# A graph layer on one core: 25 units instead of 21, 24 gathered blocks instead of 28, hand-overs set farther apart, and an opening in another order

## The reference

```python
h = jnp.maximum(_layernorm(x, axis=-1), 0.0)        # x: 12500 nodes x 128, float32
msgs = h[src]                                       # 200000 edges, sorted by dst
agg = jax.ops.segment_sum(msgs, dst, num_segments=n)
deg = jax.ops.segment_sum(jnp.ones((src.shape[0],), h.dtype), dst, num_segments=n)
agg = agg / jnp.maximum(deg, 1.0)[:, None]
h = jax.nn.relu(agg @ Wg + h @ Ws + bg)             # 128 -> 128
h = jnp.tanh(h @ W1 + b1)                           # 128 -> 512
h = jnp.tanh(h @ W2 + b2)                           # 512 -> 512
return x + (h @ W3 + b3)                            # 512 -> 128
```

## Time and profile before

| | us |
|---|---|
| median of 3 runs | 1642.91 |
| profiled execution | 1658.69 |
| its span, first to last instruction | 1656.8 |
| TensorE busy | 1257.9 (76%) |
| VectorE busy | 956.5 (58%) |
| GpSimd busy | 897.7 (54%) |
| ScalarE busy | 552.8 (33%) |

### The profile page before, as it was taken

The page is one execution under the profiler, slowest core; times in us unless marked ns, Lnnn a source line. Parts: engine busy times, 40 slices in busy tenths (PEclk is TensorE's granted clock), DMA queues, the critical chain, the costliest instruction groups (busy, mean ns, idle before and its releaser), DMA issues.

```text
span 1656.8 us, 26502 instructions
## 1 busy us (share of the span) xinstructions
PE 1257.9 (76%) x9082; PEld 924.4 (56%) x9082; DVE 956.5 (58%) x1850; ACT 552.8 (33%) x1159; POOL 897.7 (54%) x953
## 2 busy tenths in 40 slices
PE   0204988778887888877888788888887888887888
PEld 0202656556665656565655555666555656565667
DVE  8806985546555575646556574547555665546441
ACT  6303441414142341414142341424142432324152
POOL 4473165656555655656566554656555554565530
PEclk9557999999989999888999999999988889899999
DMA  9611224142413314141414313141313313141410
GB/s 244 190 51 62 79 62 100 49 99 64 87 42 100 94 44 99 45 99 41 104 49 100 92 46 93 47 102 44 103 45 101 91 45 94 47 102 43 101 41 10
DMA packets 92829, 130.44 MB, mean 79 GB/s; under 512 B 47451, under 2 KB 73393, under 8 KB 88993
## 3 DMA queue, kind: packets, MB, share of 16 engines
q1 hardware_dynamic: 63773, 69.42, 16.3%
q0 software_dynamic: 28928, 59.30, 14.4%
HBM read 109.14 MB, written 13.09 MB: 74 GB/s over the span
## 4 chain that ended last, share of the span: by engine, by line
PE 54%; another core or an unknown queue 18%; issue 12%; ACT 8%; DVE 6%; DMA 1%; DVEq 0%; SPq 0%; ACTq 0%
PE banks L870 16%; PE banks L816 14%; PE banks L741 7%; PE banks L832 5%; PE banks L853 4%; PE banks L887 4%; DVE arena L1584 3%; ACT arena L1204 2%; ACT dense L1187 2%; ACT arena L1125 1%; PE banks L844 1%; PE banks L847 1%; ACT dense L1194 1%; PE banks L789 1%
## 5 line engine op out<-in xcount | busy, mean ns | idle before, releaser
L669 POOL DMA_INDIRECT ring<-h_table,idx_all x904 | 875.6, 969 | 670.3 <-issue 235.7
L870 PE MATMUL banks<-dense,w 128*128 128x256 f32 (+1 forms) x1568 | 430.5, 392 | 30.1 <-ACT dense L1194 16.8
L816 PE MATMUL banks<-xin,arena 128*128 128x256 f16 x2058 | 313.5, 287 | 103.9 <-issue 61.3
L1204 ACT CAST arena<-banks 128x512 f16<-128x512 f32 (+1 forms) x525 | 291.7, 579 | 206.2 <-PE banks L816 129.8
L870 PEld LDWEIGHTS banks<-dense,w 128*128 128x128 f32 x1568 | 272.2, 197 | 76.7 <-ACT dense L1194 20.8
L816 PEld LDWEIGHTS banks<-xin,arena 128*128 128x128 f16 x2058 | 190.3, 102 | 217.8 <-issue 117.4
L741 PE MATMUL banks<-ring,onehot 128*128 (+1 forms) x1008 | 194.6, 290 | 23.9 <-issue 18.1
L1574 DVE TENSOR_SCALAR arena<-arena,code_ptr 128x768 f16<-128x768 f16 (+1 forms) x336 | 133.6, 456 | 119.0 <-PE banks L816 89.6
L1584 DVE TENSOR_TENSOR arena<-node,banks 128x768 f16<-128x768 f16 (+1 forms) x168 | 152.5, 965 | 45.9 <-remote 24.7
L1194 ACT ACTIVATE dense<-banks,b2c 128x256 f32<-128x256 f32 (+1 forms) x196 | 92.0, 475 | 243.5 <-PE banks L870 125.7
L832 PE MATMUL banks<-arena 64*128 64x257 f16 x2058 | 146.5, 288 | 27.1 <-issue 21.5
(11 more groups left out here) (121 smaller groups left out, 871.2 us busy)
## 6 DMA issues: line engine op xcount, KB each, us to landing
arena<-unit_codes SPq DMA_DIRECT2D x21, 1568.0 KB
ring<-h_table,idx_all POOLq DMA_INDIRECT x904
xblk<-in_x_dram SPq DMA_DIRECT2D x48, 128.0 KB
out_dram<-dense SPq DMA_DIRECT2D x48, 128.0 KB
xin<-in_x_dram SPq DMA_DIRECT2D x4, 1232.0 KB, 17.0
h_table<-xin SPq DMA_DIRECT2D x4, 1232.0 KB
own_pair<-h_table SPq DMA_TRANSPOSE x98
w<-in_L_gnn_W_dram SPq DMA_DIRECT2D x1, 1024.0 KB
```

Of the source, the lines that this page charges most:

```text
L669: nc.gpsimd.indirect_dma_start(out=ring_tiles[:, t % RING, 0:2 * D], out_offset=None, in_=table, in_offset=bass.IndirectOffsetOnAxis(ap=id ...
L816: mm = nc.tensor.matmul(to, wide_l[:, piece % WSLOTS, k, j, :], tab[:, row_of(g, j), :], start=(j == 0), stop=(j == 1))
L870: mm = nc.tensor.matmul(l3_ps[c][:, 0:w], w2[:, q, c * P:(c + 1) * P], h2T[:, q, 0:w], start=(q == 0), stop=(q == HC - 1))
L1204: nc.scalar.copy(unit_msgs[:, 2 * pr:2 * pr + wide_of, 0:2 * D], unit_ps[pr % 2][:, 0:wide_of * 2 * D].rearrange("p (g d) -> p g d", d=2 * ...
```

## The change

- PB goes from 28 to 24, so there are 25 units and 24 GpSimd blocks, and no extra blocks. Units 2 to 24 have regular periods but for period 2 and the last.
- LOT_NS is 1200, and `due` is always the clock of the last hand-over plus 1200, never less.
- OPEN_LOTS is 24. Behind the first FIRST_LOTS = 12 gathers GpSimd waits for `qlT_ready`, which ScalarE raises when unit 0's codes are ready, then issues 12 more.
- The opening: unit 0 is gathered and summed, its dense layers run at once (`first_block`) with the first two steps of GpSimd's sums, and unit 1 is prepared behind them; the first GpSimd block's layers run with the gather of unit 1 (`first_gather`); then unit 1's block with the gather of unit 2 (`period_alone(2)`).
- VectorE's work of the opening follows the same order. The splitting of the remaining source indices (`split_sources(1)`) moves behind unit 0's block.

```diff
-OPEN_LOTS = 48
-LOT_NS = 1000
+FIRST_LOTS = 12
+OPEN_LOTS = 24
+LOT_NS = 1200
-PB = 28
-EXTRA_BEHIND = (2, 4, 7, 9, 12, 14, 17, 19)
+PB = 24
+EXTRA_BEHIND = ()
+PAIRS_FIRST = (0, 0, 0, 0, 0, 0, 1, 1, 2, 2, 2, 2, 2, 2, 2, 2)
+CARRY_FIRST = 10
...
-    PERIODS, EXTRA, ORDER, pool = [((), [])], {}, [], 0
+    PERIODS, EXTRA, ORDER, pool = [((0, 1), [PB])], {}, [PB], 0
     for n in range(1, UNITS):
         if n == 1:
-            PERIODS.append(((0, 1), [PB]))
+            PERIODS.append(((2,), [0]))
+            pool = 1
+        elif n == 2:
+            PERIODS.append(((3,), [PB + 1]))
         else:
...
             spread_codes(0)
             spread_codes(1)
+            finish_block(0)
...
             for d in range(LOTS):
-                if d >= OPEN_LOTS:
+                if d == FIRST_LOTS:
+                    pool.wait_ge(qlT_ready, 1)
+                elif d >= OPEN_LOTS:
                     wait_alone(pool, lot_free, d - OPEN_LOTS + 1, issuing)
                 gather_lot(d)
...
-                    lots["due"] = max(lots["due"] + LOT_NS, lots["clock"] + LOT_NS * 3 // 4)
+                    lots["due"] = lots["clock"] + LOT_NS
...
+            def first_block():
+                steps, (block,) = PERIODS[0]
+                following = PERIODS[1][1][0]
+                leads = {}
+                def beside_layer3(slot):
+                    if slot == 7:
+                        leads[1] = begin_sums(steps[1])
+                    if slot >= 7:
+                        sum_tiles(steps[1], leads[1], range(min(2 * (slot - 7), W), min(2 * (slot - 6), W)))
+                def beside_out(slot):
+                    if slot == NT * HC - 1:
+                        for c in range(UCH):
+                            place_chunk(1, c)
+                turn(0)
+                layer1(block, 0)
+                leads[0] = begin_sums(steps[0])
+                sum_tiles(steps[0], leads[0], range(W))
+                layer2(block, 0)
+                layer3(block, 0, beside_layer3)
+                layer4(0, 2, beside_out)
+                turn(PLACE[following])
+                turn_codes(1)
+                layer1(following, PLACE[following])
...
+            def first_gather(n):
+                (step,), (block,) = PERIODS[n]
+                k = PLACE[block]
+                behind_layers = sum(PAIRS_FIRST)
+                def beside_layer3(slot):
+                    if slot == CARRY_FIRST:
+                        carry_groups(n + 1)
+                    pr = sum(PAIRS_FIRST[:slot])
+                    gather_pairs(n, range(pr, pr + PAIRS_FIRST[slot]))
+                layer2(block, k)
+                layer3(block, k, beside_layer3)
+                layer4(k, n + 2)
+                gather_pairs(n, range(behind_layers, PAIRS))
+                for c in range(UCH):
+                    place_chunk(n + 1, c)
+                segment(step)
+                turn_codes(n + 1)
+                sum_unit(n, range(NP))
...
             gather_pairs(0, range(PAIRS // 2 + 1, PAIRS))
-            for c in range(UCH):
-                place_chunk(1, c)
-            turn_codes(1)
-            end_period(0)
+            sum_unit(0, range(NP))
+            first_block()
             for n in range(1, UNITS):
                 if n == 1:
+                    first_gather(n)
+                elif n == 2:
                     period_alone(n)
```

More of the change, by code:

```diff
@@ L826, in sum_unit @@
                         pe.wait_ge(pair_taken, PAIRS * (n + 1))
-                        if not last:
+                        if n and not last:
                             pe.wait_ge(qlT_ready, n + 2)
@@ L955, in extra_block @@
                 layer1(following, PLACE[following])
+            def first_gather(n):
[15 more added lines that the diff above has]
+                turn_codes(n + 1)
+                sum_unit(n, range(NP))
             def period_alone(n):
-                steps, (unit,) = PERIODS[n]
+                (step,), (unit,) = PERIODS[n]
                 k = PLACE[unit]
-                if steps:
-                    segment(steps[0])
+                segment(step)
                 turn(k)
@@ L1235, in period @@
                 pr = 2
-                alone = is_unit(first)
-                for slot, count in enumerate(PAIRS_ALONE if alone else PAIRS_BETWEEN):
+                for slot, count in enumerate(PAIRS_BETWEEN):
                     if slot % HC == HC - 1:
                         after_layer3(first, k, [slot // HC])
-                    if slot == (CARRY_ALONE if alone else CARRY_SLOT) and n < UNITS - 1:
+                    if slot == CARRY_SLOT and n < UNITS - 1:
                         take_carry(n + 1)
-                    if slot == TURN_SLOT and not alone:
+                    if slot == TURN_SLOT:
                         take_rows(k + 1)
@@ L1245, in period @@
                     pr += count
[L1246 to L1248 removed]
+                after_layer1(unit, k + 1)
+                if n < UNITS - 1:
+                    take_q(n + 1)
                     take_codes(n + 1)
[L1250 to L1257 removed]
+                after_layer2(unit, k + 1)
+                after_layer3(unit, k + 1)
                 if n < UNITS - 1:
[L1259 removed]
+                    begin_block(behind(n))
             def begin_block(m):
@@ L1283, in _ @@
             take_pairs(0, range(PAIRS // 2 + 1, PAIRS))
+            begin_block(PERIODS[0][1][0])
+            after_layer2(PERIODS[0][1][0], 0)
+            after_layer3(PERIODS[0][1][0], 0)
             take_q(1)
+            take_rows(1)
             take_codes(1)
-            end_period(0)
+            after_layer1(PERIODS[1][1][0], 1)
             for n in range(1, UNITS):
-                period(n)
+                if n == 1:
+                    first_gather(n)
+                elif n == 2:
+                    period_alone(n)
+                else:
+                    period(n)
                 if n in EXTRA:
@@ L1653, in step, with first_gather @@
                     make_onehot(s + 2)
-            def period_alone(n):
-                steps, (unit,) = PERIODS[n]
+            def first_gather(n):
+                (step,), (block,) = PERIODS[n]
+                k = PLACE[block]
                 match_codes(n, [4])
```

155 lines of the change are left out of this document (93 added, 62 removed).

## The result

The changed kernel takes **1455.78 us** (median of 4 runs, 1454.49 to 1465.15), the kernel before on the same chip 1641.58 (4 runs, 1631.89 to 1645.46). The ratio is **0.8888 [0.8835, 0.8942]**. Faster was forecast, and by the mechanism that acted, but the time is 135 us under the forecast of 1591 and 59 under the low end of the range. The profiled execution took 1454.49 us, its span is 1452.6.

The account below looks back on a forecast made before the run. TensorE's signals arriving late while GpSimd issues gathers were taken as the bound. Span 1656.8 + 91 - 53.5 + 6 - 95 = 1605.3 us, profiled execution 1607, less 15.8 gave a median of 1591; range 1515 to 1665.

Parts of the forecast that it names:

- What bounds the kernel: Whole kernel: TensorE's signals arrive late while GpSimd issues gathers; unnamed waits hold 18%, 298 us, of the chain.
- +91: Steady part: four blocks becoming units add four regular periods and remove eight extra blocks, +91 us.
- -53.5: Opening: ScalarE's copy of unit 0's result comes at about 80.7 instead of 134.21 us, -53.5 us.
- + 6: Opening: twelve more gathers from about 82 us on bring back part of the old stall, +6 us.
- - 53: Regular periods: 32 gathers instead of 41 at 0.28 us each, 2.5 us less in each of 21 periods, -53.
- a sign of being wrong: Wrong if periods still last 66 us, `gathered` holds TensorE ahead of its sums, or unit 0's gather crawls.
- The order of the opening: Opening: the reordered work of units 0 and 1 costs 0, with 8 us either way.
- fewer gathers, farther apart: Regular periods: fewer gathers and wider spacing save 4.5 us a period, -95 us in all.
- That is nearer to the first end than to the second: Regular periods: saving lies nearer 2.5 us (price per gather stays) than 11.5 (lone gathers cost nothing); 4.5 taken.
- The third rival: Late signals nearly vanish: evenly spaced gathers never queue, periods lose nothing, -241 instead of -95, 1445 us; chance 0.12.
- +65 us: TensorE's busy time was to rise by some 65 us, 16.3 for each of four blocks made units.
- The first rival: Late signals do not go with the spacing; each period keeps its 11.5 us, 1686 us; chance 0.18.

Follow-up runs that it names:

- Experiment 1: Old hand-over rule (1000 ns, catching up to 750) put back on the changed kernel; late job 1647.4 us, ratio 0.9935; punctual job 1298.67 us, 1.0192.
- experiment 2: Changed kernel with one hand-over for two gathers, 2400 ns apart; late 1545.74 us, ratio 0.9332; punctual 1299.92 us, 1.0187.
- experiment 3: Changed kernel with 752 further TensorE increments of a semaphore nobody waits for, no gather more; late job, 1474.08 us, ratio 0.8921.
- a_oldpace2: Changed kernel with the old hand-over rule (1000 ns, catching up to 750), in a late job; 1647.4 us, ratio 0.9935 to the kernel before.
- punctual job: First job of the experiments, in which the kernel before took 1276.14 us; in all others, called late, it took 1641 to 1657.
- b_gate12: Kernel before with the wait on unit 0's codes after twelve of its 48 opening gathers, in the punctual job; 1275.53 us, ratio 0.9986.
- experiment 6: Opening's wait after twelve gathers given to the kernel before (late 1644.82 us, 0.9932) or taken from the changed kernel (late 1466.27 us, 0.8952).
- after_again: The changed kernel itself, run again beside the kernel before in a late job; 1479.25 us, ratio 0.8922.
- a_oldpace: Changed kernel with the old hand-over rule (1000 ns, catching up to 750), in the punctual job; 1298.67 us, ratio 1.0192 to the kernel before.
- a_lot2: Changed kernel with one hand-over for two gathers, 2400 ns apart, in the punctual job; 1299.92 us, ratio 1.0187 to the kernel before.
- a_nogate: Changed kernel without the wait after twelve gathers, its 24 opening gathers in one run, in the punctual job; 1307.66 us, ratio 1.0252.
- a_ns1240: Changed kernel with LOT_NS 1240 instead of 1200, in a late job; 1475.32 us, ratio 0.8909 to the kernel before.
- a_nogate2: Changed kernel without the wait after twelve gathers, its 24 opening gathers in one run, in a late job; 1466.27 us, ratio 0.8952.

## Why the prediction was right, and where it was wrong

**What bounds the kernel: right.** Signals of TensorE that come late while GpSimd issues gathers made up the difference. Experiment 1 shows it by taking the close gathers back, experiment 2 by pairing them, and experiment 3 shows that it is not TensorE's increments.

**The units, the opening and the smaller number of gathers: right in sum, by errors that cancel.** `a_oldpace2` is the change without its spacing. It measured -0.65% of 1656, -10.8 us. The prediction's terms for it are +91 - 53.5 + 6 - 53 = -9.5. That closeness is luck. By the same terms unit 4's copy was due at 268.6 and came at 294.9, 26 us late; twenty periods of 66.3 - 2.5 = 63.8 us lasted 62.8, 19 us less; and the end took 90.7 us instead of 102.7. In the punctual job the exchange of blocks for units costs nearly nothing: by the windows of `b_gate12` a regular period is 47.6 us and an extra block 23.6, so 4 x 47.6 - 8 x 23.6 = +2. So most of the 91 hangs on the late signals.

**The opening: right on the copy, short on what follows.** 80.5 us for the copy is as forecast, and unit 0's gather did not crawl. But "-53.5" is no price of the gate: on the kernel before, the same gate brings 10 us, since 36 gathers behind it hold the pair signals (experiment 6). It needed the shorter opening too. Unit 4's copy was due at 249.8 + 66.3 - 53.5 + 6 = 268.6 and came at 276.6, 8 late. Most of it is TensorE's wait for a gathered tile, which the prediction had named as a sign of being wrong. The changed kernel:

```profile
193.10 0.94 POOL L675 DMA_INDIRECT ring<-h_table,idx_all  x1 [0.30 <-issue]
...
200.54 0.82 PE L749 MATMUL banks<-ring,onehot 128*128 x3 [7.29 <-issue]
```

The chain follows that gather from 193.10 to 199.53. `after_again` waits 6.97 us at the same place, and `a_oldpace2`, with the old rule, has no such wait: the spacing costs some 7 us there.

The order of the opening costs more than 0, too. In the punctual job unit 4's `q_sb` copy of `a_oldpace` comes at 249.4 and unit 3's of `b_gate12` at 188.4. These are 61.0 us, and the regular period between them is 47.6: 13 us more, where 0 with 8 either way was said.

**The spacing: the failed step.** The term "fewer gathers, farther apart" was -95 us, 4.5 us a period, of which 2.5 were for the smaller number and 2.0, or 42 us, for the spacing. "That is nearer to the first end than to the second" was wrong. A period became 12.3 us shorter, and in one and the same job the spacing alone is worth 7.7 us a period (62.8 to 55.1) and 168 us in all. Against 61.8 us forecast, twenty periods of 54.0 make -156 us; the opening gives +8 and the end -5 (95.5 for 1605.3 - 268.6 - 20 x 61.8 = 100.7), and together they are the 153 us between forecast span and measured span (1605.3 and 1452.6). The third rival, 1445 us with a chance of 0.12, came nearest in time, but not for its reason alone: it had a period lose nothing, and 2.4 us of the 11.5 are still unnamed (48 us in twenty periods; 7.6% of the chain, 4.2 us, in `after_again`), while 4.2 us of shorter busy time, which it did not have, more than made up for it. Three readings led me astray:

- I set the spacing, 1.2 *nominal* us, against a service time of 1.25 *real* us and found that GpSimd "does not rest". But the same paragraph had 44 nominal us in a period that takes 66.3. On average 1.2 nominal us are then 1.2 x 66.3 / 44 = 1.8 real ones; and in the changed kernel a gather starts 1.29 us (median) behind its hand-over's end, where it was 2.33 before.
- Against the third rival I held that gathers ran at 60% of the full rate and that half of them cannot have queued. 60% is GpSimd's busy share; at 1.25 us each, 769 gathers are 75% of 1279 us. And of the 767 hand-overs of that stretch only 43 found GpSimd with nothing else in hand, while 439 found two or more gathers unfinished. In the changed kernel's steady part 112 of 639 did.
- I multiplied a mean price, 0.28 us a gather, by a count. The price goes with the queue. The table gives how late TensorE's next signal is in the steady part: mean us from the modelled end of its matmul to the next event of its semaphore (number of signals), by the gathers that GpSimd had not finished when the hand-over came.

| gathers ahead | before | `a_oldpace2` | changed kernel | `a_oldpace`, punctual |
|---|---|---|---|---|
| none | 0.02 (40) | 0.02 (70) | 0.04 (55) | 0.01 (49) |
| one | 0.60 (270) | 0.40 (267) | 0.64 (444) | 0.02 (102) |
| two | 1.17 (286) | 1.13 (259) | 0.77 (86) | 0.03 (220) |
| three | 1.70 (101) | few | few | 0.05 (269) |

These are rough: signals without an event within 15 us, 49 of 767 before and 33 to 44 of 640 in the next two, are left out. But on the late occasions a signal with nothing ahead is on time and each gather ahead makes it later, and what the spacing altered is above all how often two or three stand there.

**TensorE's busy time: wrong sign.** +65 us was said, -17.6 measured. The matmuls are there (9890 for 9082), but the granted clock is 0.98 where it was 0.92 in the steady part, and the same matmuls take less time. Of the 12.3 us a period, 4.2 are this (53.6 to 49.4 busy), which no term of the sum had; the other 8.1 are idle time of TensorE that went. The clock explains at most 3.2 of the 4.2 (49.4 x 0.98 / 0.92 = 52.6); what the rest is was not found. That fewer stalls raised the clock is likely, since the two go together here, but no run changes one alone.

**The first rival** (late signals stay whatever the spacing) is refuted by experiment 1, where the spacing alone is worth 168 us. The page behind it, the Trainium skill's "TensorE: Matmul & The Clock Gate", section "The cost: per-tile semaphore tail", puts the completion increments of matmuls that are packed as tiles of the array at about 26 ns each. By that, 752 more are at most 20 us as an estimate; experiment 3 measured none that shows (0.8921 against 0.8922). So an increment is no dearer here than the page has it, but its price is no bound on how late a signal can land: the copy that hung on one in the opening before came 53.5 us after its matmul.

**Left open.** What the delay physically is, and what decides between a punctual and a late occasion. When gathers move, their DMA packets move with them, and no experiment parts GpSimd's issuing from that traffic; the last window of this document has a signal outstanding with neither at work. The changed kernel itself was not run on a punctual occasion; the variants of it that were lose 1.9% (`a_oldpace`, `a_lot2`) and 2.5% (`a_nogate`) there. So the gain of 11% holds where signals are late. No kernel that beats the changed one was found: `a_ns1240` is level with it.

## What to carry to other kernels

When a chain of waits has a large unnamed share on a single core, look at what GpSimd does in those moments: here, setting the gathers on average farther apart than GpSimd needs for one, with no catching up, was worth 168 us, and the rest of the change, with a seventh of the gathers gone, 11. Look under "issue" as well, since late signals can hide there. Price such a delay by how many requests stand in a queue, not by a mean per request, and turn a planner's nominal times into real ones before they are compared with a service time. And time a change beside its parent in several sessions: here the edit is worth -11% on one occasion, and its nearest variants cost 2% on another.

## What the hardware showed that was not expected

- The same kernel took 1276 us in one job and 1641 to 1657 in the others, with the same work. The first job kept no trace of that kernel, but the four traces that it has show no wait by "remote"; in `b_gate12`, level with it, a regular period is 47.6 us instead of 66.3. Kernels of one job always agreed on which of the two it was. The chip's number does not tell: a later job on a chip with the number of the first had late signals.
- A semaphore update of TensorE can land long after its matmul: in the opening of the kernel before, the two increments behind matmuls that ended at 79.40 and 80.66 us landed at 106.85 and 134.19, and GpSimd was issuing gathers from 63.15 to 126.1 us. The second landed 8.1 us behind the last gather, and for 6 of these no engine and no DMA was at work, as this window has it:

```profile
128.00:134.00 6.00, 0.00 (x0) 0.00 (x0) 0.00 (x0) 0.00 (x0) 0.00 (x0) 0.50 0.00 0
```

  In `a_nogate2` the copy comes 4.3 us behind the last gather. So a delayed signal is not released at once when the gathers stop.
- Where signals are late, the trace has fewer events of a semaphore than increments of it: 747 of `lot_free` for 856 before, 637 for 752 in the changed kernel, but 748 for 752 in the punctual `a_oldpace`. Whether several landed as one or the records were lost was not found.
- One gather of 128 rows costs GpSimd 0.94 to 0.95 us (median) and 0.30 to the next in the traces of all jobs, so the delay is not in GpSimd's own pace.
